# Two cross-attention layers in one program: maxima end earlier, ring slots are reloaded earlier, side jobs are paced by bank

## The reference, cut to what matters

```python
# layer 0: x (4, 512, 320), context (4, 1024, 512), 20 heads of 16, text = first 1020 tokens, ip = last 4
q, k_t, v_t = heads(x @ W_q), heads(text @ W_k), heads(text @ W_v)
probs_t  = softmax(q @ k_t.T * 0.25)
text_out = probs_t @ v_t
qsem     = l2norm(probs_t @ text)            # (heads, queries, 512): the large product
sem      = qsem @ l2norm(ip).T
probs_ip = softmax(q @ k_ip.T * 0.25 + 0.5 * sem) * mask
x1       = (text_out + probs_ip @ v_ip) @ W_out + b_out + x
# layer 1: text = first 77 tokens, ip = the other 947
out = (softmax(q1 @ k1.T * 0.25) @ v1 + softmax(q1 @ k1_ip.T * 0.25) @ v1_ip) @ Wo.T + bo + x1
```

## Time and profile before

| | us |
|---|---|
| median of 3 timed runs | 3947.04 (3946.88 to 3949.18) |
| profiled execution | 3935.86 |
| its span, first to last instruction | 3934.0 |
| TensorE matmul busy | 3554.4 (90%) |
| VectorE busy | 2124.6 (54%) |
| ScalarE busy | 1696.6 (43%) |
| GpSimd busy | 1078.1 (27%) |

### The profile page before, as it was taken

The page is one execution under the profiler, slowest core; times in us unless marked ns, Lnnn a source line. Parts: engine busy times, 40 slices in busy tenths (PEclk is TensorE's granted clock), DMA queues, the critical chain, the costliest instruction groups (busy, mean ns, idle before and its releaser), DMA issues.

```text
span 3934.0 us, 66570 instructions
## 1 busy us (share of the span) xinstructions
PE 3554.4 (90%) x24208; PEld 2942.0 (75%) x24208; DVE 2124.6 (54%) x5503; ACT 1696.6 (43%) x3724; POOL 1078.1 (27%) x889
## 2 busy tenths in 40 slices
PE   6999899988998989998999888999899999999767
PEld 3787778876887768887788776888678788888434
DVE  4444345455555555555555454565555556555676
ACT  0332223443444434444444444444345455555444
POOL 2111110323232222233232222322323322222333
PEclk7999999999999999999999999999999999999877
DMA  4235422324334212232333612223233622222222
GB/s 144 61 92 54 88 73 58 96 53 60 60 62 98 49 45 64 65 109 70 54 66 54 101 43 49 68 69 96 68 57 69 54 52 53 54 48 47 49 55 43
DMA packets 636270, 260.59 MB, mean 66 GB/s; under 512 B 491852, under 2 KB 591004, under 8 KB 635938
## 3 DMA queue, kind: packets, MB, share of 16 engines
q1 hardware_dynamic: 635944, 256.33, 30.4%
HBM read 199.96 MB, written 55.44 MB: 65 GB/s over the span
## 4 chain that ended last, share of the span: by engine, by line
PE 80%; DVE 8%; issue 7%; DMA 2%; SPq 1%; ACT 1%; POOL 0%; DVEq 0%; ACTq 0%
PE acc L886 8%; PE acc L879 8%; PE acc L881 7%; PE acc L882 7%; PE acc L887 7%; PE acc L880 6%; PE score L849 4%; PE spare L930 3%; PE av L917 3%; PE score L930 3%; PE score L851 3%; PE av L921 3%; PE score L966 2%; PE spare L966 2%; PE score L1002 1%
## 5 line engine op out<-in xcount | busy, mean ns | idle before, releaser
L1071 ACT ACTIVATE prob<-score 128x512 f32<-128x512 f32 x1219 | 730.2, 599 | 1839.9 <-PE score L851 1837.7
L1371 POOL TENSOR_TENSOR prob_lo<-prob,prob_hi 128x512 fp32r<-128x512 f32 x593 | 791.0, 1335 | 1737.6 <-ACT prob_hi L1074 1737.3
L879 PE MATMUL acc<-tok_v,prob_hi 128*128 128x300 f32 x2240 | 925.3, 413 | 6.5 <-DMA tok_v<-v_scr 5.8
L881 PE MATMUL acc<-tok_lo,prob_hi 128*128 128x256 f32 (+1 forms) x2560 | 779.1, 304 | 0.4 <-POOL tok_lo L1400 0.4
L886 PE MATMUL acc<-tok_v,prob_lo 128*128 128x278 f32 (+1 forms) x2560 | 757.9, 296 | 7.6 <-DVE prob_lo L1134 7.6
L882 PE MATMUL acc<-tok_lo,prob_hi 128*128 128x256 f32 (+1 forms) x2560 | 729.6, 285 | 0.0
L887 PE MATMUL acc<-tok_v,prob_lo 128*128 128x256 f32 (+1 forms) x2560 | 728.0, 284 | 0.0
L1074 ACT ACTIVATE prob_hi<-score 128x512 fp32r<-128x512 f32 x1219 | 724.5, 594 | 0.0
L880 PE MATMUL acc<-tok_v,prob_hi 128*128 128x256 f32 x2240 | 634.3, 283 | 0.0
L1134 DVE TENSOR_TENSOR prob_lo<-prob,prob_hi 128x512 fp32r<-128x512 f32 x687 | 502.9, 732 | 102.8 <-ACT prob_hi L1074 102.5
L849 PE MATMUL score<-q_ring,k_ring 99*128 99x256 bf16 (+1 forms) x1219 | 344.5, 283 | 196.7 <-issue 188.0
(11 more groups left out here) (253 smaller groups left out, 5031.7 us busy)
## 6 DMA issues: line engine op xcount, KB each, us to landing
k_ring<-k_scr SPq DMA_DIRECT2D x960, 64.0 KB
tok_v<-v_scr SPq DMA_DIRECT2D x160, 176.0 KB, 3.4
v_ring<-v_scr SPq DMA_DIRECT2D x160, 148.5 KB, 3.3
ctx_t<-in_ctxT SPq DMA_DIRECT2D x8, 2048.0 KB, 9.4
q_ring<-q_scr SPq DMA_DIRECT2D x960, 16.0 KB
v_scr<-v_stage SPq DMA_DIRECT2D x32, 440.0 KB, 2.5
k_scr<-part_bf SPq DMA_DIRECT2D x32, 384.0 KB, 2.5
v_scr<-v_stage SPq DMA_DIRECT2D x36, 330.0 KB, 8.6
```

Of the source, the lines that this page charges most:

```text
L879: e.matmul(out_a[:, 0:SEG + VCOLS], p_hi, tok_v[0:kk, c, seg, v_lo:v_lo + SEG + VCOLS], start=first, stop=False)
L881: e.matmul(out_a[:, t0:t0 + SEG], p_hi, tok_lo[0:kk, c, seg * SEG:(seg + 1) * SEG], start=False, stop=False)
L1071: e.activation(prob[:, es, :], bank_s[:, :], ACT.Exp, scale=SCALE)
L1371: e.tensor_tensor(prob_lo[:, ps, :], prob[:, es, :], prob_hi.bitcast(F32)[:, ps, :], ALU.subtract).then_inc(s_low[1], 1)
```

## The change

The margins grow from 5 to 6, from 8 to 11 and from 11 to 16 steps, and `max_rows` comes 1 step after `neg` in place of 2. A clause for all groups but the first of the last unit keeps a margin from going far beyond what the group before it in the layer has: `last_at` is not earlier than 7 steps after the last one's, as long as 7 steps of margin are left. Loads are put 2 steps (1 in the lead) ahead of the end of the group in the slot, no earlier than 28 (lead 25, tail 36) steps before the group's start in place of 24 (tail 32), and they wait for the exponentials of that group's last step (`s_exp`) and no longer for its products (`s_main`). Side jobs wait for 2 slots since a job ended on the bank `o.banks[-1]` only, not since any job ended.

```diff
-MAX_SPAN = {"lead": (8, 5), "woven": (11, 8), "tail": (8, 11)}
+MAX_SPAN = {"lead": (8, 6), "woven": (11, 11), "tail": (8, 16)}
-    def maxima(g, rest=2):
+    def maxima(g, rest=1):
...
-            at = max(end_of[g - RING], start_of[g] - (24 if start_of[g] < tail else 32))
+            done_at = end_of[g - RING] - (1 if end_of[g - RING] < woven else 2)
+            at = max(done_at, start_of[g] - (25 if g < RING + 12 else 28 if start_of[g] < tail else 36))
...
-    slot_no, rest_until = [0], [0]
+    slot_no, bank_ended = [0], {}
...
         if seq[g] == (2 * B - 1, 0):
             last_at = start_of[g] - 7
+        else:
+            last_at = max(last_at, min(latest_at.get(UNITS[seq[g][0]][0], 0) + 7, start_of[g] - 7))
...
         for _ in range(limit):
             if not current:
                 due = bool(urgent and urgent[0][0] <= now[0])
-                if not due and not topq and not bgq or slot_no[0] < rest_until[0] and len(topq) + len(bgq) + due < BACKLOG:
+                if not due and not topq and not bgq:
                     return
+                if slot_no[0] < bank_ended.get(o.banks[-1], -SPACING) + SPACING and len(topq) + len(bgq) + due < BACKLOG:
+                    return
+            jobs_so_far = len(o.job)
             run_step()
-            if not current:
-                rest_until[0] = slot_no[0] + SPACING
+            if not current and jobs_so_far:
+                bank_ended[o.banks[0]] = slot_no[0]
...
                     if free_before_load[g]:
-                        e.wait_ge(s_main, free_before_load[g])
+                        e.wait_ge(s_exp, free_before_load[g])
```

## The result

The changed kernel takes **3735.79 us** (median of 4 runs, 3732.28 to 3741.95), the kernel before 3948.11 on the same chip (4 runs, 3946.88 to 3955.72). The ratio is 0.946, 95% interval 0.9442 to 0.9478: 5.4% less, where 5.5% and 3730 us were forecast.

The account below looks back on a forecast made before the run. TensorE's work plus 380 us of idle time, led by waits for the maxima's rows, was taken as the bound. Gains of -254 and costs of +37 gave -217: 3719 us profiled, 3730 us median, range 3672 to 3815.

Parts of the forecast that it names:

- lead, idle and clock: Lead: its score-line waits of 16.2 us go (-16), and the better clock gives -6.
- The rows: Score line L849: "issue" waits are for the maxima's rows; maxima 4 steps earlier remove all 150.1 us in the woven stretch.
- Rival A: Rows freed by half only, as the shift is 1 or 2 steps: 3857 us, or 3832 with fewer costs; chance 0.12.
- The clock: TensorE's work lost at the lower clock level after waits: -60 us woven (bounds 45 and 75), lead -6, tail -4.
- The costs: New TensorE waits in the woven stretch: +3 for loads, +8 for `neg`, +26 for banks, together +37 us.
- The banks: TensorE's wait for banks ahead of max jobs: +26 us over 38.1, bounds -15 and +115; idle ahead of L930 60 to 80.
- Rival C: Bank waits replace row waits, 4051 to 4307 us; they outweigh the gain from 0.20 us per job; chance 0.03.
- the +3 and +8 for loads and `neg`: Woven stretch: max jobs waiting for ring loads, +3 us (0 to +20); `max_rows` sooner after `neg`, +8 (0 to +40).
- SyncE's wait: SyncE at ring loads: 229 us of waits for layer-1 products shrink to under 60 us at L1470 with `s_exp`.
- The load edit: Ring loads 2 to 4 steps earlier on `s_exp`: no longer stand in front of row DMAs; cost +3 us.
- The pacing: Pacing by bank: jobs start in successive slots, a bank returns after two; +26 us in the woven stretch.
- Tail: Score-line waits fall by 8 us, L917's by 10, clock gives 4: -22, bounds 0 and -45.

Follow-up runs that it names:

- experiment 4: Kernel before, with row DMAs writing to a memory scratch and TensorE not waiting for the maxima's rows: 3707.95 us, ratio 0.9374.
- experiment 1: Kernel before with only the maxima moved: larger margins, `max_rows` one step after `neg`, the `last_at` clause; old loads and pacing: 3763.13 us, ratio 0.9515.
- experiment 9: Changed kernel with the old ring loads and their wait for products, and a woven margin of 9 in place of 11: 3736.48 us, ratio 0.9453.
- experiment 6: Changed kernel with the old ring loads and their wait for products; maxima and pacing changed: 3726.49 us, ratio 0.943.
- experiment 5: Changed kernel with the old pacing (2 slots after any job); maxima and ring loads moved: 3736.07 us, ratio 0.9453.
- experiment 2: Kernel before with only the ring loads moved earlier and waiting on `s_exp`: 3893.7 us, ratio 0.9844.
- experiment 7: Changed kernel with the old margins and rest, so only ring loads and pacing changed: 3953.2 us, ratio 0.9998.
- experiment 8: Changed kernel with ring loads at their new places but waiting for the products (`s_main`) again: 3816.66 us, ratio 0.9659.
- experiments 11: Changed kernel plus 5-slot side-job stop after a unit's `combine`, later layer-1 q projection, and value load ahead of ring loads in the tail: 3710.4 us, ratio 0.9391.
- experiment 12: Changed kernel with old ring loads and product wait, plus 5-slot stop after `combine` and value load first in the tail: 3711.06 us, ratio 0.9388.

## Why the prediction was right, step by step

| step | forecast | measured |
|---|---|---|
| woven, waits at the score line by "issue" | -150 | -150.1 (none left) |
| woven, new costs (loads 3, `neg` 8, banks 26) | +37 | +44 |
| woven, clock | -60 | -43.5 |
| lead, idle and clock | -16, -6 | -15.5, -11.5 |
| tail | -22 | -25 |
| profiled execution | -217 | -202.3 |

The +44 is 150.1 less the 106.4 us by which the woven stretch's idle time fell.

**The rows: right.** The "issue" wait at L849 falls from 188.0 us to 11.3 in the whole execution, 10.7 of them in the tail, and to 18.1 with the wait that the profile now names after the rows' DMA; under 25, mostly in the last 200 us, was the mark. Experiment 4 shows that the wait was for the rows, experiment 1 that the maxima alone take nearly all of it away (26.1 us left). Rival A, the half gain, is wrong in a useful way: its premise was tried in experiment 9, and half the shift did not give half the gain. The waits were each at most 7.9 us long, and only 4 of the 66 in the woven stretch were longer than 2 steps of 2.87 us. Pricing a partial shift in proportion was the error in that rival. But the waits' length against the shift isn't the whole of it either: by that, 3 us of them should be left, and 27.1 are. The time hardly shows it, because other waits are shorter there: TensorE's idle time is 242.3 us, and 239.8 in experiment 6.

**The clock: right in sum, mis-sized by stretch.** For the whole execution 60 + 6 + 4 = 70 us were forecast, and TensorE's busy time fell by 65.8 (3554.4 to 3488.6). The woven term was too large by 16 and lies just under its bound of 45; lead and tail together gave 22 in place of 10. The record of the granted clock in the two traces shows where the woven term went wrong. The stretch ran at the lower level for 191 us before (its mean clock is 0.968; the 177 come from the rounded 0.97) and for 75 us after (0.987). Matmuls filled 152 of the 191 us, a share of 0.79, where the four samples gave 0.67, and 61 of the 75. The samples are the longest wait and waits of 5.3, 4.4 and 2.4 us, not the two longest. So the lower level cost 76 us before, more than the 59 of the forecast, and 30 us of it stay, where the forecast let all go. Half of the fall in the time that matmuls filled at the lower level is 46 us for the woven stretch against 43.5 measured, 67 for the whole execution against 65.8, and 62 for experiment 4 against 62.9.

The Trainium skill ("TensorE: Matmul & The Clock Gate", Terms) would price the woven stretch at half of (191 - 75), an estimate of 58 us, and experiment 4 at half of the fall in time at the lower level, 389 to 208 us, which is 91 us. Measured were 43.5 and 62.9. In both places that rule takes the idle time inside the slow stretches for lost work.

**The costs: right in sum, wrong in their parts.** The banks cost 57.0 - 38.1 = +19 us, near the +26 and just under the mark of 60 to 80. Some 11 of the 19 are of the pacing (experiment 5 has 45.7). Rival C's point of 0.20 us per job is far off. But 22 us come from a wait that I had not priced: TensorE for `x_in`, 4 times in the woven stretch. SyncE's timeline of the changed kernel shows the place. A ring load comes just ahead of the next projection's DMAs, and its 14 issues hold them up for 8 us:
```profile
1429.13 0.50 SPq L1540 DMA_DIRECT2D x_scr<-closing  x1
1429.74 0.75 SPq L1480 DMA_DIRECT2D k_ring<-row_scr  x2
...
1437.03 0.42 SPq L1485 DMA_DIRECT2D q_ring<-q_scr  x1
1437.62 0.34 SPq L1435 DMA_DIRECT2D x_in<-x_scr  x1
...
1442.49 0.77 PE L956 MATMUL score<-x_in,w_q 128*128 128x256 f32 x1 [6.47 <-DMA x_in<-x_scr]
```
The runs show that it takes the moved loads and the pacing together. TensorE's waits for `x_in` in the woven stretch are 6.0 us with the loads alone (experiment 2), 9.0 with loads and maxima (5), 2.9 with maxima and pacing (6), and 21.8 with loads and pacing (7). In the order that `plan()` writes out, the first matmul of these four projections stands 2 scores behind its loads, where it was 6 to 10 before the change and is 4 to 6 in experiment 6. It is 1 or 2 in experiment 2 as well, so this distance is the work of the loads, and what the pacing adds was not traced.

Another 10.7 us are waits of L927 for GpSimd's `prob_lo`. Against these stand the +3 and +8 for loads and `neg`: no max job waits for its load in the woven stretch, and L946 waits 0.8 us there for `neg_max` (8.6 in the tail). The step that failed is thus the move of the loads: I priced what waits for the load itself, and not the other DMAs that it is moved past. And I priced each edit for itself, where this cost comes of two.

**SyncE's wait: wrong.** It was to fall below 60 us at L1470, and it is 383.1. Experiment 2 shows the reasoning was sound for the old order (5.9 us): there SyncE waits 792.8 us for the split of the rows (`max_bf`) and reaches the load late. In the changed kernel that wait is 208.1 us, SyncE runs ahead of TensorE and reaches the load before the exponentials. No first score of the woven stretch waits, since the rows now land some 11 us (median) ahead of their score. With the products' wait instead, the same place costs 80 us (experiment 8).

**The load edit: not needed.** I had counted it as +3 and expected experiment 6 to be slower without it. Alone it brings 1.6%, beside the earlier maxima and without the pacing (experiment 5 against 1) it brings 0.6%, and with both it brings nothing and may cost 0.3% (experiment 6; the intervals just touch). A reason that fits the rows, not tested by itself: it frees SyncE for the row DMAs, which no longer are late, and pays with the waits for `x_in`.

**The pacing: not settled.** Alone -0.3%, with the loads alone +1.5% (experiment 7 against 2), with the maxima alone about -0.9% (6 against 1), and on top of both nothing (the change against 5). Idle time at max jobs rises with it in the absence of the earlier maxima (45.5 to 89.8 us, experiments 2 and 7). Why the score line's waits rise with it too was not traced. The edits' effects don't add, so its price depends on what else stands in the order.

**Tail: right in sum.** Forecast were 18 us of waits and 4 of clock; measured are 14 of idle time and 11 of clock. The score line gave 4 us and not 8: its waits are 17.5 us of the 21.7, since the first three groups of the last unit still wait 15.5. The 10.46 us wait for a value load behind three ring loads stays, as forecast, and L917's waits fall from 25.2 to 10.6 (15 forecast); that of 10.6 for `x_in` is now 8.6. VectorE's busy time in the whole execution is 2116.4 us, nearly as before (2124.6).

**Luck.** The forecast took the median 11.2 us above the profiled execution, as before; after the change it is 2.2 above. The profiled time was forecast 15 us too low (3719), the median only 6. The sums of the clock and of the costs came out for a like reason: woven 16 us too much and lead and tail 12 too little, and 22 us for `x_in` where 11 for loads and `neg` did not come and the banks cost 7 less.

## What to carry to other kernels

When an engine's wait nearly always ends the same short time after a DMA's last issue (1.09 to 1.14 us here), it is probably the DMA that it waits for, whatever the profile's "issue" says; a run without the wait, as experiment 4, settles it. Here it was cheap to put the producer earlier by more than the longest wait, and half of that shift was nearly as good. Price a moved DMA by every transfer behind it in its queue, and ask what it waits for at its new place. Edits that relieve the same wait don't add: try the one that removes the wait alone before the others are kept.

## What the runs showed of the hardware

VectorE's small casts of the maxima take 214 to 217 ns in the median and up to 1197 for the same instruction. The long ones stand beside GpSimd's work, and end when it ends: in the changed kernel 44 of the 320 casts last over 0.36 us, and each of them ends 76 to 81 ns behind a GpSimd instruction. In the timeline of the changed kernel a cast of 4 rows of 128 starts 0.14 us after a GpSimd subtraction and ends 0.07 us behind it; the subtraction after it likewise lasts as long as GpSimd's next one (1.27 us, where its median is 0.28):
```profile
1612.47 1.17 POOL L1383 TENSOR_TENSOR part_r<-part_f,part_bf 128x512 f32<-128x512 f32 x1 [4.92 <-DVE part_bf L1151]
1612.61 1.10 DVE L1262 CAST max_bf<-max_t 4x128 bf16<-4x128 f32 x1
1613.59 1.28 POOL L1377 TENSOR_TENSOR prob_lo<-prob,prob_hi 128x512 fp32r<-128x512 f32 x1
1613.75 1.27 DVE L1264 TENSOR_TENSOR max_r<-max_t,max_bf 4x128 f32<-4x128 f32 x1
```
The Trainium skill ("SBUF — State Buffer", section "SBUF: two separate sides") describes this: VectorE and GpSimd share one pair of ports, and whichever holds it keeps the other out for its whole instruction. Of VectorE's instructions the page counts those in a 2-port mode and those with two inputs in SBUF. The subtraction above has two such inputs, and the rows agree; whether the cast runs in a 2-port mode no run here shows.

A second cause of long bank waits was not in the prediction either. The two longest waits of max jobs in the changed kernel (4.73 us) stand behind VectorE's work at the end of a unit, during which no bank is emptied:
```profile
1122.25 1.88 DVE L1309 TENSOR_TENSOR heads_out<-heads_out,small 128x640 f32<-128x640 f32 x1
1124.17 0.82 DVE L1311 TENSOR_TENSOR attn<-attn,heads_out 128x640 f32<-128x640 f32 x1
1124.91 0.68 DVE L1239 TENSOR_REDUCE max_parts<-score 128x1 f32<-128x512 f32 x1
...
1125.65 0.61 PE L936 MATMUL score<-k_ring,q_ring 96*128 96x512 bf16 x1 [4.73 <-DVE max_parts L1239]
```
This is what the stop of 5 slots in experiments 11 and 12 addresses. In experiment 12 no max job waits longer than 2.2 us for `max_parts`; two waits for `closing`, of 5.9 and 5.4 us, stay there, as in experiment 6 (5.9 and 6.2).
